# ScalarE makes part of a weighted operand of the graph matrices that VectorE made alone

## What is computed

```python
msgs = h[src]
agg = jax.ops.segment_sum(msgs, dst, num_segments=x.shape[0])        # layers 0 and 2
norm = dinv[row] * ew * dinv[col]
out = jax.ops.segment_sum(h[row] * norm[:, None], col, num_segments=n)   # layer 3
```

## Time and profile before

| | |
|---|---|
| median of three timed runs | 3201.57 us |
| lowest and highest of them | 3198.20 and 3201.84 us |
| profiled execution, its own time | 3204.95 us |
| span of its instructions | 3202.9 us |
| stretch of the building stage | 56 to 674 us |

### The profile page before, as it was taken

The page is one execution under the profiler, slowest core; times in us unless marked ns, Lnnn a source line. Parts: engine busy times, 40 slices in busy tenths (PEclk is TensorE's granted clock), DMA queues, the critical chain, the costliest instruction groups (busy, mean ns, idle before and its releaser), DMA issues. The chain is left out here.

```text
span 3202.9 us, 66923 instructions
## 1 busy us (share of the span) xinstructions
PE 2664.1 (83%) x21196; PEld 2401.5 (75%) x21197; DVE 1703.1 (53%) x3605; ACT 1365.3 (43%) x2809; POOL 909.0 (28%) x1144
## 2 busy tenths in 40 slices
PE   3888888869999997688777777787787868959999
PEld 2877778759999995676666666666666657749999
DVE  7877787773443446544444444444444452355465
ACT  2544444423333334344444444444444420217676
POOL 2121221200000000566656665666556500000000
PEclk7999999979999998555555555555555569879999
DMA  2333333320000002434334343433334360028172
GB/s 68 116 102 101 101 113 103 102 75 2 2 2 2 2 2 82 118 105 102 103 100 106 101 101 101 106 103 101 103 103 105 94 261 2 1 118 342 56 267 78
DMA packets 221032, 300.28 MB, mean 94 GB/s; under 512 B 101187, under 2 KB 186662, under 8 KB 215430
## 3 DMA queue, kind: packets, MB, share of 16 engines
q1 hardware_dynamic: 181926, 217.20, 21.4%
q0 software_dynamic: 38880, 79.68, 9.8%
HBM read 225.96 MB, written 70.80 MB: 93 GB/s over the span
## 5 line engine op out<-in xcount | busy, mean ns | idle before, releaser
L1128 POOL DMA_INDIRECT layer_R<-source_terms,layer_srcs x804 | 765.9, 953 | 504.8 <-DVE layer_zp L1172 280.2
L1329 PE MATMUL layer_zp<-layer_Wa,layer_at 64*128 64x192 f32 x1620 | 597.0, 536 | 239.7 <-issue 234.8
L1329 PEld LDWEIGHTS layer_zp<-layer_Wa,layer_at 64*128 64x128 f32 x1620 | 489.7, 323 | 295.2 <-issue 283.6
L535 PE MATMUL build_win<-nodes_x,build_S 128*128 128x200 bf16 x5264 | 503.9, 253 | 125.4 <-DVE nodes_x L452 119.4
L535 PEld LDWEIGHTS build_win<-nodes_x,build_S 128*128 128x128 bf16 x5264 | 444.0, 99 | 181.3 <-DVE nodes_x L452 117.9
L930 PE MATMUL layer_acc<-layer_U,graph_CT 128*128 128x192 f16 x6250 | 522.0, 247 | 19.2 <-DVEq L760 19.2
L930 PEld LDWEIGHTS layer_acc<-layer_U,graph_CT 128*128 128x128 f16 x6250 | 517.8, 98 | 26.9 <-issue 22.9
L1172 DVE TENSOR_TENSOR layer_zp<-layer_zp,layer_R 128x1152 f32<-128x1152 f32 x135 | 183.8, 1361 | 306.5 <-remote 306.3
L1353 PEld LDWEIGHTS layer_acc<-layer_hot,layer_G 128*98 128x98 f32 x1644 | 286.5, 287 | 69.3 <-issue 65.4
L1353 PE MATMUL layer_acc<-layer_hot,layer_G 128*98 128x32 f32 x1644 | 292.4, 349 | 48.8 <-issue 31.6
L1280 ACT ACTIVATE layer_y<-layer_zp 128x1152 f32<-128x1152 f32 x135 | 152.7, 1131 | 379.7 <-DVE layer_zp L1172 352.4
(11 more groups left out here) (243 smaller groups left out, 3004.8 us busy)
## 6 DMA issues: line engine op xcount, KB each, us to landing
layer_ring<-W_blocks SPq DMA_DIRECT2D x41, 1600.0 KB, 7.9
W_blocks<-nodes_x SPq DMA_DIRECT2D x400, 100.0 KB, 1.8
layer_at<-in_attr SPq DMA_DIRECT2D x135, 192.0 KB
C_blocks<-build_Cblk SPq DMA_DIRECT2D x25, 800.0 KB, 3.6
layer_C<-C_blocks SPq DMA_DIRECT2D x25, 800.0 KB, 21.5
layer_rows<-target_rows SPq DMA_DIRECT2D x135, 144.0 KB
layer_R<-source_terms,layer_srcs POOLq DMA_INDIRECT x804
layer_Qs<-target_terms SPq DMA_DIRECT2D x135, 36.0 KB
```

The costliest lines, as they stand in the source:

```text
L535: mm = pe.matmul(out, S[:, b, part, 2 * i + u, :, :].rearrange("p a z -> p (a z)"), M[:, i, u, :, :].rearrange("p a z -> p (a z)"), start= ...
L1128: nc.gpsimd.indirect_dma_start(R[:, h, u, :], None, P_d, bass.IndirectOffsetOnAxis(ap=at_u, axis=0)).then_inc(s_R[h], 16)
L1329: mm = pe.matmul(out[u], at[:, h, u * P:(u + 1) * P], Wa[:, :], start=(u % 2 == 0), stop=False, skip_group_check=True)
```

## The change

Version 3 of the source operands is split. VectorE makes it for the edge tiles 0 to 5 of a group, ScalarE for the tiles 6 to 9. ScalarE first copies the four weight parts of its tiles from bf16 to an fp32 tile `scale`, waits for its own copy, and then makes one scaled copy of 128 elements per tile. It does so after the second window of each group, for the group that follows; for group 0 it does it ahead of everything. A semaphore `s_third` counts two per group. TensorE waits for it ahead of a group's third window, the first that can read tile 6. SyncE waits for it before it overwrites the weight parts of that buffer. Apart from this `residual_gcn` drops the semaphore `s_id` and counts the same event on `s_c`.

```diff
+        scale = m.sb("scale", [P, 2, GT - 6], F32)
...
+        s_third = m.sem("last_third_parts_made")
...
                             sp.wait_ge(s_sw, (g + 2) * 16)
                             sp.sem_inc(s_taken, 1)
+                            sp.wait_ge(s_third, 2 * g + 2)
+                            sp.sem_inc(s_taken, 1)
                             columns(u // GW % 2, g + 2)
...
-                nc.vector.tensor_tensor(S[:, bass.ds(b, 1), 1 + part, :, :, :].rearrange("p o t a z -> p (o t) a z"),
-                                        S[:, bass.ds(b, 1), 0, :, :, :].rearrange("p o t a z -> p (o t) a z"),
-                                        sw[:, bass.ds(b, 1), 1 + part, :, :].rearrange("p o t z -> p (o t) z").unsqueeze(2).to_broadcast(TILE),
+                end = 6 if part == 2 else GT
+                nc.vector.tensor_tensor(S[:, bass.ds(b, 1), 1 + part, 0:end, :, :].rearrange("p o t a z -> p (o t) a z"),
+                                        S[:, bass.ds(b, 1), 0, 0:end, :, :].rearrange("p o t a z -> p (o t) a z"),
+                                        sw[:, bass.ds(b, 1), 1 + part, 0:end, :].rearrange("p o t z -> p (o t) z").unsqueeze(2).to_broadcast([P, end, P // 2, 2]),
                                         ALU.mult)
...
                         pe.wait_ge(s_made, w + 1 + 2 * GW)
+                        if i == 2:
+                            pe.wait_ge(s_third, 2 * g + 2)
                         products(q % 2, i, range(FEW - 1))
...
+            def third(b, g):
+
+                act.wait_ge(s_hot, g + 1)
+                act.wait_ge(s_third, 2 * g)
+                nc.scalar.activation(scale[:, b, :], sw[:, b, 3, 6:, 0], ACT.Copy).then_inc(s_third, 1)
+                act.wait_ge(s_third, 2 * g + 1)
+                for t in range(6, GT):
+                    one = nc.scalar.activation(S[:, b, 3, t, :, :].rearrange("p a z -> p (a z)"),
+                                               S[:, b, 0, t, :, :].rearrange("p a z -> p (a z)"), ACT.Copy,
+                                               scale=scale[:, b, t - 6:t - 5])
+                one.then_inc(s_third, 1)
+
...
                     nc.scalar.activation(Wwin[:, u % 4, :], win[:, u % 4, WC:2 * WC], ACT.Copy).then_inc(s_evac, 1)
+                    if u % GW == 1:
+                        third((u // GW + 1) % 2, j * (WPT // GW) + u // GW + 1)
...
             act.wait_ge(s_ready, 2)
+            third(0, 0)
             node_tile(0, 0, False)
```

More of the change, by code:

```diff
@@ L1409, in residual_gcn @@
         s_c = m.sem("iotas_made")
-        s_id = m.sem("identity_made")
         s_v = m.sem("dve_chain")
@@ L1460, in _ @@
             do(nc.vector.memset(mask[:, 0, :], 1.0))
-            nc.vector.tensor_scalar(mask[:, 1, :], mask[:, 1, :], float(LAST), None, ALU.is_lt).then_inc(s_id, 1)
+            nc.vector.tensor_scalar(mask[:, 1, :], mask[:, 1, :], float(LAST), None, ALU.is_lt).then_inc(s_c, 1)
             layernorm_relu(nc, do, root(1), x[:, :, :], h[:, :, :], stat, cv[:, :, :])
@@ L1531, in _ @@
         def _(pe):
-            pe.wait_ge(s_id, 1)
+            pe.wait_ge(s_c, 3)
             pe.wait_ge(s_par, 16 * 5 * NL)
```

## The result

The changed kernel takes 3211.76 us, the median of 8 runs from 3208.32 to 3215.55, beside 3202.07 us for the kernel before (8 runs, 3198.20 to 3203.95). The ratio is 1.0031, with an interval of 1.0022 to 1.0040. It is slower, by 9.7 us. The forecast was 3202.0 us with a range up to 3210, so the time lies 1.8 us above the range.

The account below looks back on a forecast made before the run. No engine is full in the matrix-building stage; VectorE works a fixed list with TensorE behind it. VectorE -0.27 and SyncE +0.7 sum to +0.4 us on the 3201.57 median: 3202.0 us, range 3194 to 3210.

Parts of the forecast that it names:

- VectorE, 0 us: Last weighted multiply of each group: 0.266 us shorter, but idle time already follows it, so 100 steady groups gain 0.
- the rival in which the gain comes through: VectorE's instruction stream is held by its datapath, so the shorter multiply gains 8.2 us (3193.4 us); chance 0.1.
- The part on ScalarE, 1.5 us: Per group, four copies of about 0.31 us end to end plus 0.25 for the scales; bounds 1.05 and 1.9 us.
- TensorE is not held by late evictions: Building stage: evictions may be about 3 us late and lag less, so TensorE loses 0 us.
- a lag of 1.7 and 1.1: After ScalarE's part and a turned piece in a row, the next two evictions start 1.7 and 1.1 us late.
- SyncE, the columns' DMA, 0.7 us with 0 and 5 as bounds: Source columns go out later behind the group's last window store; total cost taken as 0.7 us, bounds 0 and 5.
- the worst place is the second window of a tile's second group: There eviction, new part and turned piece stand in a row on ScalarE: 2.87 us against a window of 1.12.
- a shift of 1.2 us costs 0 to 0.2 us: Normal column transfers land about 1 us before the one-hots need them, so later issue costs at most 0.2 us.
- if that is why the columns are late, a later issue meets less of it: Six late fourth-group landings: if an instruction transfer of 1.2 us delays them, later issue loses nothing, otherwise some 5 us.
- The added waits of SyncE and TensorE: Per group, SyncE's wait and increment take 0.15 us at most; TensorE's wait costs 0 to 2 us, taken as 0.
- the second one, ScalarE's lag reaches VectorE: With 1.9 us for ScalarE's part, late evictions delay the columns past their margin: 3215 us; chance 0.2.
- from 13 to over 20: Sign that ScalarE's lag reaches VectorE: the one-hots' waits for the columns' DMA rise from 13 to over 20.

Follow-up runs that it names:

- both kernels with the columns first: Changed kernel and kernel before, each with SyncE issuing source columns ahead of the group's last window store: 2947.02 and 2947.22 us, beside 2953.42 for before.

## Why the prediction was wrong, point by point

- *VectorE, 0 us.* Right. The idle time ahead of the target step grew from 0.5 to between 0.77 and 0.80 us in the groups named, "issue" from 14.5 to 27.6 us, and with ScalarE's part the long and the short multiply give the same time (3210.66 and 3210.53 us), as do both kernels with the columns first. The runs settle these differences to some 3 or 4 us, so 0 is shown only to that; the 8.2 us of the rival in which the gain comes through are out.
- *The part on ScalarE, 1.5 us.* Right in the sum, 1.42 us, and partly by luck in its terms: I counted four copies of 0.31 us end to end, where each takes 0.390 us and they overlap. The row of a copy with a constant scale had 283 ns for 96 elements, and the copies with a scale from SBUF take 390 ns for 128 and start 0.292 us apart. The Trainium skill (ScalarE: Activation LUTs, section What ACT_TABLE_LOAD costs) states the terms of an estimate, 186 + 0.833 x 128 + 93 = 386 ns, and an overlap of 93 ns. The trace agrees with both (390 ns, and 390 - 292 = 98 ns of overlap).
- *TensorE is not held by late evictions.* Right: 3 waits of it for L624, 1.7 us in all. The eviction of window 6 starts 1.39 us behind its matmuls (0.15 before) and that of window 7 0.79 us, where a lag of 1.7 and 1.1 was expected.
- *SyncE, the columns' DMA, 0.7 us with 0 and 5 as bounds.* This is the step that failed, three times over. First, the working named one place, "the worst place is the second window of a tile's second group", and priced the columns of the fourth group alone. The same coincidence of part and turned piece stands at window 9, and delays window 11 (0.86 us) and the columns of the next position, by 0.95 us. It brought nine of the 13 new late one-hots. Second, the sentence "a shift of 1.2 us costs 0 to 0.2 us" took the margin of about 1 us as one number. It is a spread: the start of the one-hots differs by group, and with the median margin at these two positions at 0.4 to 0.5 us after the shift (1.1 to 1.4 before) a landing slow by some tenths is already late. Third, "if that is why the columns are late, a later issue meets less of it": a later issue can as well meet what it was ahead of before. The group at 150 us is one such, and slow landings (over 2.9 us) at the first position went from 1 to 6, while their total went from 32 to 29. The collisions moved, and they moved to where no margin was left.
- *The added waits of SyncE and TensorE.* Right at about nothing: with the part behind the first window they are all there, and the time is that of before. The issue of that kernel is 0.02 to 0.05 us later, less than the 0.15 us that I allowed. At the second position, behind the store of the tile, the issue is 0.56 us later where 0.1 was expected. Its late one-hots stayed at 11 and 9, so it cost nothing that is seen here. Most of it is there already when the tile's own store is issued, 1.70 us behind the window at the median against 1.28; what delays that store isn't shown.
- *The rivals.* What happened is the second one, ScalarE's lag reaches VectorE, with its sign: waits for the columns "from 13 to over 20", measured 20 and 23. It was said to decide from 1.4 us for the new part on, and the part took 1.42. It was priced at 13 us, for a part of 1.9 us; it cost 8.6 to 9.7 us with one of 1.42 us. With my own 1.5 us I was inside its condition, and still gave it 0.2 of the chance, since I took the shift as covered.

By the ends of TensorE's windows, the 18 groups whose one-hots are late after and weren't before are longer by 13.7 us together, as much as the stage; seven that are no longer late give back 1.4 us, and the other 74 together lose 1.5. Single groups differ by 1 us and more between two traces of the unchanged kernel, so no group is a measurement by itself.

What stays open: how much of the 9.7 us is plain lateness and how much collisions with instruction transfers wasn't told apart.

## What to carry to other kernels

A helper engine with idle time still has places where two of its jobs stand in a row. Ask there not only whether the main engine is held, but which DMA is issued behind the late step, how much margin its landing has at the worst of its positions, and repeat the sum for every position where the two jobs meet. A busy-time gain counts for nothing where the shortened instruction already has idle time behind it. And a transfer that is needed early should be issued ahead of transfers that nobody waits for: here that alone was worth 6 us, where the change itself had nothing to give.

## What the runs showed of the hardware

- A transfer of instructions is one packet of 16 KB. The stage before has 100 of them, and each keeps one of the 16 DMA engines for 0.9 to 1.8 us (1.1 at the median). The 20 KB load's own first packet starts 1.35 us after its issue, and the load lands in 2.3 us. Outside the second position it was slow 11 times, 3.0 to 3.6 us, and each time such a packet had begun between the issue and the load's first packet; that was so for only 2 of the 63 others (2.7 us). After, it was so for 11 of 15 slow landings, and the other four, the slowest (3.8 to 4.4 us), met one that began up to 1.1 us behind the load's first packet.
- Slow landings of the columns (over 2.9 us) were 32 of 100 before, 21 of them at the second position, behind the 800 KB store of a tile. With the columns issued about 1 us earlier, and ahead of that store, there were none, at the same traffic.
- The price of lateness is not proportional. By 0.4 to 0.6 us it cost 3 us in the whole program, by 1.0 us 8.6 to 9.7, by 0.9 to 1.5 us 20 (there the stores moved too).
- In the five groups in which TensorE's program comes round its loop (16 groups of code), TensorE stands idle for 3.8 to 5.0 us ahead of the first matmul, though VectorE made its operand 3.6 to 4.7 us earlier. Counted by the ends of its windows these groups take 9.8 to 14.9 us each against 5.1 for an undisturbed one, and their sum over a trace varied from 58 to 69 us. In single traces of this kernel that is as large as the effect looked for.
